# Second distances: the squared distance less its root's square formed on TensorE, 14 of their units beside the first alignment and 18 beside its way back

## What is computed

```python
def _pairwise_euclidean(a, b):
    aa = jnp.sum(a * a, axis=-1)[:, None]
    bb = jnp.sum(b * b, axis=-1)[None, :]
    ab = a @ b.T
    return jnp.sqrt(jnp.maximum(aa + bb - 2.0 * ab, 0.0))
...
def col_step(left, inp):
    d_ij, up, diag = inp
    r = d_ij + jnp.minimum(jnp.minimum(up, left), diag)
    return (r, r)
...
def _align_one(small, large):
    D = _pairwise_euclidean(small, large)
    R = _dtw_cost(D)
    i_idx, j_idx, valid = _backtrack(R, T_small, T_large)
    contrib = small[i_idx] * valid[:, None].astype(small.dtype)
    expanded = jnp.zeros((T_large, d), dtype=small.dtype).at[j_idx].add(contrib)
    return expanded
...
x = x + _L0_xattn_ref(ctx_1024, _layernorm(x, axis=-1))
x = x + _L0_attn_ref(_layernorm(x, axis=-1), ...)
x = x + _L0_ffn_ref(_layernorm(x, axis=-1), ...)
```

## Time and profile before

| | us |
|---|---|
| median of 3 runs | 1205.58 |
| lowest and highest | 1204.58, 1206.51 |
| the profiled execution | 1209.82 |
| its span, first to last instruction | 1208.6 |
| busy in it: PE, DVE, ACT, POOL | 995.0, 700.1, 478.0, 115.5 |
| first distances, from its start | about 15 to 152 |
| forward steps of the first alignment, with second distances | 162.8 to 295.6 |
| way back, with second distances until 374.6 | 295.6 to 388.6 |
| second alignment begins | 392.0 |

### The profile page before, as it was taken

The page is one execution under the profiler, slowest core; times in us unless marked ns, Lnnn a source line. Parts: engine busy times, 40 slices in busy tenths (PEclk is TensorE's granted clock), DMA queues, the critical chain, the costliest instruction groups (busy, mean ns, idle before and its releaser), DMA issues.

```text
span 1208.6 us, 15659 instructions
## 1 busy us (share of the span) xinstructions
PE 995.0 (82%) x4836; PEld 591.7 (49%) x4836; DVE 700.1 (58%) x2434; ACT 478.0 (40%) x839; POOL 115.5 (10%) x150
## 2 busy tenths in 40 slices
PE   5885649888560699987797599888799999999998
PEld 2332213333220355453575365646576767676776
DVE  5984859999899477478569802346522222222226
ACT  4884626766661244423331155242122222222221
POOL 1000000000000000000000000000233434342210
PEclk9997979999875799989898899788899999999999
DMA  9999854447785879540050089195121312123115
GB/s 356 327 292 291 233 157 150 145 151 169 238 211 139 266 243 318 173 140 30 0 173 9 0 279 291 58 332 219 46 65 43 98 44 92 55 86 106 37 44 183
DMA packets 123520, 190.06 MB, mean 157 GB/s; under 512 B 8848, under 2 KB 92976, under 8 KB 123440
## 3 DMA queue, kind: packets, MB, share of 16 engines
q1 hardware_dynamic: 117552, 170.70, 46.2%
q0 software_dynamic: 5888, 18.36, 5.0%
HBM read 165.00 MB, written 24.03 MB: 156 GB/s over the span
## 4 chain that ended last, share of the span: by engine, by line
PE 55%; DVE 28%; DMA 7%; issue 4%; ACT 3%; SPq 3%; POOL 0%; DVEq 0%; ACTq 0%; POOLq 0%
PE bank L1766 13%; PE bank L1613 8%; PE bank L1799 7%; PE bank L1758 4%; PE bank L1634 4%; DVE table L787 4%; DMA spaced<-dist 4%; PE bank L1778 3%; PE bank L1791 3%; DVE beyond L803 2%; DVE passed L808 2%; DVE z L729 2%; DVE col_min L780 2%; DVE z L721 2%; PE bank L1558 2%
## 5 line engine op out<-in xcount | busy, mean ns | idle before, releaser
L989 DVE TENSOR_TENSOR hid<-bank,act_s 128x352 f32<-128x352 f32 x104 | 54.2, 524 | 201.9 <-PE bank L1766 159.1
L1766 PE MATMUL bank<-w_up,srcT 128*128 x512 | 162.9, 460 | 0.6 <-ACT srcT L1405 0.6
L1542 PE MATMUL bank<-sq,ones 128*64 128x402 f32 (+1 forms) x512 | 104.3, 530 | 43.9 <-ACT sq L1272 43.9
L1413 ACT ACTIVATE act_s<-bank 128x352 f32<-128x352 f32 x104 | 48.0, 463 | 222.5 <-PE bank L1766 121.5
L1536 PE MATMUL bank<-ctxT,latT 128*64 128x402 f32 (+1 forms) x512 | 105.2, 534 | 20.6 <-DMA ctxT<-ctx_tr_dram 19.8
L1558 PE MATMUL bank<-table,ident 128*128 128x402 f32 x144 | 66.6, 545 | 65.4 <-DVE stays L757 56.0
L1766 PEld LDWEIGHTS bank<-w_up,srcT 128*128 128x128 f32 x512 | 96.0, 189 | 47.7 <-issue 3.9
L1272 ACT ACTIVATE sq<-ctxT 128x1608 f32<-128x1608 f32 x64 | 97.5, 1526 | 16.0 <-DMA ctxT<-ctx_tr_dram 16.0
L1613 PE MATMUL bank<-rows_c,on_path 128*64 128x256 f32 (+1 forms) x832 | 99.9, 392 | 0.9 <-DMA rows_c<-ctx_nat_dram 0.4
L1799 PE MATMUL bank<-w_dn,hidT 128*128 (+1 forms) x384 | 93.5, 380 | 0.4 <-DVE y_sb L1010 0.4
L1305 ACT ACTIVATE code<-bank,unpassed 128x402 bf16<-128x402 f32 x72 | 42.1, 590 | 122.7 <-PE bank L1560 122.7
(11 more groups left out here) (285 smaller groups left out, 1636.2 us busy)
## 6 DMA issues: line engine op xcount, KB each, us to landing
rows_c<-ctx_nat_dram SPq DMA_DIRECT2D x32, 896.0 KB
ctxT<-ctx_tr_dram SPq DMA_DIRECT2D x32, 804.0 KB, 8.5
ctxT<-ctx_tr_dram SPq DMA_DIRECT2D x32, 797.0 KB, 8.8
rows_c<-ctx_nat_dram SPq DMA_DIRECT2D x32, 640.0 KB
spaced<-dist SPq DMA_DIRECT2D x128, 101.0 KB, 4.7
w_up<-w_t_dram SPq DMA_DIRECT2D x16, 704.0 KB, 13.1
table<-spaced SPq DMA_DIRECT2D x16, 404.0 KB, 11.5
table<-spaced SPq DMA_DIRECT2D x32, 202.0 KB, 5.7
```

The lines of the kernel that those rows point to most:

```text
L989: e.tensor_tensor(hid[i][:, :], psum[2 * i + 1][:, 0:HH], act_s[i][:, :], ALU.mult).then_inc(hid_done, 1)
L1542: last = e.matmul(ps[b * T:(b + 1) * T, 0:nq], ones[:, 0:T], sq[i][:, b, k, 0:nq], start=False, stop=(k == KC - 1))
L1766: last = e.matmul(psum[2 * i + m][:, 0:HH], srcT[t % 2][:, k, :], w_up[:, bass.ds(ex, 1), m, k, columns], start=(k == 0), stop=(k == KC - 1))
```

## The change

For the second units alone, the difference z - root2 is no longer formed by VectorE. TensorE forms it with two products, the identity with z and the negated identity (`less`) with root2, in bank 3 or 4, and VectorE multiplies that bank by the slope. The new `distance_left(u)` waits for ScalarE's root2 of unit u and for VectorE's product of unit u - 2. VectorE's product waits for `left_over` and the slope.

The interleaving changes as well. A unit is now two pieces on all three engines, and `beside_first` gives the count of alignment pieces behind each: 3 and 2 for the first 14 units (FORWARD_UNITS), then 2 and 2 or 2 and 1 in turn. So 14 units stand beside 70 of the 72 forward pieces, 18 beside the rest and 61 steps of the way back, and 10 steps are left behind the last unit. On TensorE the products of unit u + 1 stand between the two new products of unit u - 1 and of unit u. The first distances and SP's program stay as they are.

```diff
--- before.py
+++ after.py
@@ -65,6 +65,8 @@
 LW = L + 1
 DISTS = 4
 
+FORWARD_UNITS = 14
+
 TIE = 2.0 ** -36
 PASSED = 4096.0
 HALVES = 2 * CODES
...
@@ -219,6 +221,19 @@
 def rows_value(n):
 
     return sum(16 if m // 2 % 2 == 0 else 32 for m in range(n + 1) if rows_slot(m) == rows_slot(n))
+
+
+def beside_first(n):
+
+    u, second = divmod(n, 2)
+    if u < FORWARD_UNITS:
+        return CB - 2 if second else CB - 1
+    return 1 if second and u % 2 else 2
+
+
+def refined_value(u, part):
+
+    return 2 * u + part if u < GUNITS else GUNITS + u + 1
 
 
 def behind_second(n):
...
@@ -717,20 +732,23 @@
             def distance_refine(u):
                 i, nq = u % 2, unit_rows(u)
                 zi, sl = z[i][:, 0:nq], slope[i][:, 0:nq]
+                if u >= GUNITS:
+
+                    e.wait_ge(slope_act, u + 1 - GUNITS)
+                    e.wait_ge(left_over, u + 1 - GUNITS)
+                    e.tensor_tensor(zi, psum[3 + i][:, 0:nq], sl, ALU.mult).then_inc(refined, 1)
+                    return
                 e.wait_ge(rooted, 2 * (u + 1))
                 e.tensor_tensor(zi, zi, root2[i][:, 0:nq], ALU.subtract).then_inc(refined, 1)
-                if u < GUNITS:
-                    e.tensor_scalar(sl.bitcast(I32), root2[i][:, 0:nq].bitcast(I32), -0.5, HALF_RSQRT_MAGIC, ALU.mult,
-                                    ALU.add).then_inc(slope_dve, 1)
-                    e.wait_ge(slope_dve, u + 1)
-                else:
-                    e.wait_ge(slope_act, u + 1 - GUNITS)
-                e.wait_ge(refined, 2 * u + 1)
+                e.tensor_scalar(sl.bitcast(I32), root2[i][:, 0:nq].bitcast(I32), -0.5, HALF_RSQRT_MAGIC, ALU.mult,
+                                ALU.add).then_inc(slope_dve, 1)
+                e.wait_ge(slope_dve, u + 1)
+                e.wait_ge(refined, refined_value(u, 1))
                 e.tensor_tensor(zi, zi, sl, ALU.mult).then_inc(refined, 1)
 
             def distance_add(u):
                 i, nq, slot = u % 2, unit_rows(u), u % DISTS
-                e.wait_ge(refined, 2 * (u + 1))
+                e.wait_ge(refined, refined_value(u, 2))
                 if u >= DISTS:
                     e.wait_ge(dist_out[slot], dist_slot_value(u - DISTS))
                 else:
...
@@ -741,6 +759,9 @@
                 for u in range(g * GUNITS, (g + 1) * GUNITS):
                     if g == 0:
                         distance_bias(u)
+                    else:
+
+                        yield
                     if u > g * GUNITS:
                         distance_refine(u - 1)
                         distance_add(u - 1)
...
@@ -1295,6 +1316,8 @@
                 for u in range(g * GUNITS, (g + 1) * GUNITS):
                     if u + 1 < (g + 1) * GUNITS:
                         squares(u + 1)
+                    if g:
+                        yield
                     distance_roots(u)
                     yield
 
...
@@ -1567,11 +1590,26 @@
                 for step in range(STEPS):
                     yield
 
+            def distance_left(u):
+
+                i, nq = u % 2, unit_rows(u)
+                e.wait_ge(rooted, 2 * u + 2)
+                if u >= GUNITS + 2:
+
+                    e.wait_ge(refined, refined_value(u - 2, 2))
+                e.matmul(psum[3 + i][:, 0:nq], ident[:, :], z[i][:, 0:nq], start=True, stop=False)
+                e.matmul(psum[3 + i][:, 0:nq], less[:, :], root2[i][:, 0:nq], start=False, stop=True).then_inc(left_over, 1)
+
             def distances(g):
 
-                for u in range(g * GUNITS + 1, (g + 1) * GUNITS):
-                    distance_products(u)
-                    yield
+                for u in range(g * GUNITS, (g + 1) * GUNITS):
+                    if u > g * GUNITS:
+                        distance_left(u - 1)
+                    yield
+                    if u + 1 < (g + 1) * GUNITS:
+                        distance_products(u + 1)
+                    yield
+                distance_left(u)
 
             def path_weigh(n):
                 pair = n // 2
...
@@ -1938,7 +1976,7 @@
                 if u in LATENTS_AT:
                     latents(LATENTS_AT[u])
             distance_products(GUNITS)
-            interleave(distances(1), align(0), lambda n: CB)
+            interleave(distances(1), align(0), beside_first)
             interleave(align(1), chain(add_rows(range(0, 4)), together(recurrence(0), add_rows(range(4, 8))),
                                        beside(recurrence(1), experts(RUNS[0]), shared_beside), experts(RUNS[1])),
                        behind_second)
```

More of the change, by code:

```diff
@@ L475, in build @@
         z_dve, z_act, rooted, refined = sem("z_dve"), sem("z_act"), sem("rooted"), sem("refined")
-        slope_dve, slope_act, dist_done = sem("slope_dve"), sem("slope_act"), sem("dist_done")
+        slope_dve, slope_act, left_over, dist_done = (sem(n) for n in ("slope_dve", "slope_act", "left_over", "dist_done"))
         dist_out = [sem(f"dist_out{i}") for i in range(DISTS)]
```

## The result

Beside four runs of the kernel before, with a median of 1206.05 us (1204.58 to 1207.7), the changed kernel takes **1218.41 us** (1216.14 to 1221.43, four runs): ratio 1.0093, 95% interval 1.0072 to 1.0115. It is slower by about 1%. (The ratios and intervals here are those on record; they can differ a little from the quotient of two medians, which is 1.0102 here.) Its profiled execution took 1221.43 us with a span of 1220.2, 11.6 us more than the profiled execution before (1208.6).

What follows compares the result with a forecast made beforehand. VectorE, 94% busy beside the forward steps, was taken to bound the kernel up to the last distance. That distance, at 384.6 instead of 374.6 us, moved the 1205.6 us median by 10 us to 1215.6, given as 1215.5, range 1196 to 1221.

Steps and rivals of the forecast that it cites:

- case F: Way back: the late context slot blocks VectorE; +2 to +15 us, time 1215.5 us; chance 0.62.
- Forward steps: First alignment: TensorE paces at 8.46 us a round, forward steps take 124.4 us and end at 287.2 us.
- Load and slot: Way back: large table load issued about 304 us, 16 us later; context slot 27.3 us after it, at 331.3.
- Who holds VectorE: Unit 53: VectorE's product waits for new TensorE products behind unit 54's; before, it needed only ScalarE's root.
- The wait for unit 53: Way back: VectorE stands still some 13 us; unit 53 finished at 338.3 us, unhindered at 325.
- Ten units: Way back after unit 53: ten units at TensorE's 4.41 us each, 44.1 us, reaching 382.4 us.
- The last slot: Behind a second table load: 19.8 us against 17.6 of four units, so +2.2 us, up to 6.
- After the last distance: Second alignment starts 17.3 us after the last distance, decided by the table's last load; everything later moves by 10 us.
- R1: Way back: slot hidden if within about 14 us of the load's issue, TensorE paces; -5.4 us, 1200; chance 0.15.
- R2: Whole stretch to the last distance: VectorE's work alone counts; -16.7 us, 1189; chance 0.08.
- R4: Way back: TensorE idles repeatedly at lower clock, stores hold dist's ring; second wait over 6 us; +15 to +25, 1225; chance 0.06.
- R3: Gains and losses cancel: forward steps end at 279.5, slot two or three us quicker; within 2.4 us of 1205.6; chance 0.09.

## Why the prediction was right, and where its sizes were off

The forecast was 1215.5 us by case F, with 1207.5 to 1220.5 as its own range; the median is 1218.41. That the late slot holds VectorE is shown from three sides: a smaller load gives 10.6 us back, another order within the engines 6.6, and both together bring it 15.4 us below the changed kernel. Through which engine it does so the forecast had only in part, and there it was lucky. Step by step:

- **Forward steps.** Forecast 8.46 us a round by TensorE; five rounds from 183.87 to 226.03 are 8.43 each. Forecast length 124.4, end 287.2; measured 124.3 and 287.44.
- **Load and slot.** Forecast load at 304 and slot 27.3 us after, at 331.3; measured 303.86 and 27.6, 331.49. The slot was read as one measured interval, from the load's issue to the slot's use, and moved whole. That held, though its parts shifted by a microsecond each: the slot was issued 7.6 us behind the load instead of 8.6, and was there 20.0 us behind its own issue instead of 18.7.
- **Who holds VectorE.** The prediction says that before the change VectorE's work "does not need the late products", and takes the whole wait for one that the new pair adds. This reading is wrong. ScalarE's squares stand before the same slot and ahead of the root, so VectorE was held in the kernel before as well, and got off with 1.31 us because it came to the unit only 2 us after the slot had landed. In the changed kernel it came 9.3 us before the slot, and by these rows 12.5 of the 16.8 us would have been waited without the pair. What makes the wait long is thus the load's later issue, which the split brings; the pair's place adds 4.3 us. The date came out right because the sum went from the slot by way of TensorE's products and pair, which do end last.
- **The wait for unit 53.** Forecast 13 us, measured 16.8. Unhindered the unit would have been finished at 322.2 + 1.2 = 323.4 rather than 325. For unit 48 to unit 53 the sum had taken TensorE's 4.41 us a unit, but before the slot TensorE was ahead and VectorE's own pace of 4.2 us counted, from 302.4 on instead of 303; this makes the wait longer, not the date later. The date is later by the next term: from the slot to the pair 337.04 - 331.49 = 5.55 us instead of 4.68, and from there to VectorE's product 1.97 instead of 1.34, for the whole stretch was at the low clock (granted 0.50 from 323 to 335 us). The 4.68 of the earlier trace rows ends within the recovery of a shorter stop. VectorE's two operations took 1.19 us instead of 0.94. Unit 53 is finished at 340.2, forecast 338.3: +1.9.
- **Ten units.** Forecast 44.1 us. Measured without the second wait 388.4 - 340.2 - 6.6 = 41.6. TensorE's unit is 4.38 (343.19 to 347.57), as forecast, but by two errors that cancel: the pair costs 1.53 us and not 1.34, the products 2.85 and not 3.07. And the last unit follows 1.9 us after the one before it, because TensorE had worked ahead while VectorE stood: -2.5.
- **The last slot.** Forecast +2.2, up to 6; measured 6.6. This is the term that was mis-sized most. From unit 57's add (357.7) to the slot's issue are 2.9 us instead of 1.3: SP was still issuing the second table load, whose issue alone takes 4.20 us (355.10), and the store came only at 359.34. The sum had moved the queue but had not counted that SP's own issuing takes time. From the slot to VectorE's product of unit 61 are 380.5 - 373.4 = 7.1 us instead of 6.0, for the products, at the low clock again, took 5.36 us. And the sum had left out VectorE's own 1.2 us behind that, which it had counted for unit 53.
- **After the last distance.** Forecast: all later dates 10 us later, and later stages keep their lengths. Measured: last distance +13.8, second alignment (first scan) 402.84 against 392.36, +10.5, first row sums 424.60 against 410.57, +14.0, first routed expert 881.6 against 870.0, +11.6. The prediction had the table's last load decide when the second alignment begins, 17.3 us after the last distance. That was not so before: the load is issued at 377.68 there, and in the changed kernel, where VectorE does wait for it (1.35 us), it is used 11.0 us after its issue. In the kernel before it was VectorE's own 15 steps that ended last, without a wait. With 10 steps the load decides, 14.1 us after the last distance, and 3.3 us are saved. The row sums do not gain by that: the context rows are asked for behind the last table load, at 396.01 instead of 382.24, and carry the 14 us on. Between the row sums and the experts 2.4 us came back.

So F was right in kind and 4 us short in the last distance, of which 2 were given back later. R1 is what the two cures come near to, though its condition isn't met even there: the slot is used 18.4 us behind the load's issue, not within 14, and with the pair ahead the time is 1203, 3 us above the 1200 worked out, for waits of 7 us are left. R2 is refuted by the forward steps, where TensorE sets the pace. R4's own sign, a second wait of over 6 us, did come with 6.6 us at unit 61, and TensorE worked at the lower clock after both stops, as R4 says; what did not come in the changed kernel is a wait for dist's ring, and the size stays below R4's +15. The ends of F and R4 were thus not told apart by that sign. R3 is refuted twice: the forward steps end at 287.4 and not 279.5, and the slot was not quicker.

The product from a bank: forecast no dearer than from SBUF. Measured 0.55 to 0.58 us for 402 columns, against 0.57 for the same operation from SBUF. The Trainium skill (VectorE: DVE Perf Modes, the section on the TRN2 errata) gives PSUM sources a fixed term of 120 cycles against 58; no row here shows such a difference. By an estimate from the page's figures it would be 65 ns, which would be seen in these rows. What the forecast left out altogether is ScalarE; the kernel with the split alone, whose wait of 8.8 us names ScalarE's root, shows the same.

## What to carry to other kernels

When work is moved from one engine to another, look at what the new engine does between the parts that the old one needs: an in-order engine that stands before a late transfer now holds back everyone who waits for results queued behind it. Look in the same way at every engine that feeds the unit: here ScalarE's order accounts for the larger part of the long wait, and a short wait in the profile before (1.31 us) had already named it. Read the time from a load's issue to its use as one interval and move it whole, then add the issuing time of the queue itself and take the products at the clock of an engine that has just stood. The cure here was twofold, a smaller transfer ahead of the wanted one and the finishing work issued before the wait, on each engine that shares the wait; either alone gave half to most of the loss back, and both together turned it into a small gain over the kernel before, though not one shown against that kernel with the same smaller load.

## What the runs showed of the hardware

- A table load and a context slot behind it kept all 16 transfer engines full while they moved only 230 GB/s (304 to 323 us), and 340 GB/s once the context came (323 to 335 us). Half the table load (two pairs instead of four) shortened the time from its issue to the slot's use from 27.6 to 18.2 us; with three pairs, in the kernel with the loads moved, it was 26.7 us.
- After 14.5 us without work TensorE's products ran at a granted clock of 0.50, the 1.2 GHz level: eight products in 2.95 us, and 1.57 us once it was back. The stop of 3.23 us in the kernel with both cures left the first products nearly at full speed (1.64 us, granted clock 0.94), but the eight behind them took 2.95 us (0.50), so the lower clock can also set in only behind the first products. After 3.86 us (373.43), and after 3.11 us in the kernel before (340.44), the first eight already took 2.95, and after 3.92 us in the kernel with the halved load they took 1.67: the length of the stop alone doesn't tell which.
- Issuing a load of the table kept SP's queue for 4.2 us with nine transfers of 202 KB (355.10) and for 6.2 us with nine of 404 KB (303.86). A store and a slot that were ready to be asked for in the meantime came behind it. In the kernels with moved loads 202 KB each took 4.9 and 5.6 us too; what sets the issuing time was not tested.
